# A sandwich layer on one core: three biases moved from TensorE to VectorE and GpSimd, idle matmuls in the second batch, a new order of slots

## What is computed

```python
x_proj = (ln(x) @ w_in.T + b_in)             # q, k, v; the values' bias is bv
opt = softmax(q @ k.T / 4).sum(keys) * v     # per head; see below
x = x + ln(opt @ w_out.T + b_out)
h = ln(x); base = h @ wi_W.T + wi_b
inter = relu(base + (h @ lora_A[i].T) @ lora_B[i].T)   # i = argmax of the gate
x = x + ln(inter @ wo_W.T + wo_b)
```

## Time and profile before

| | us |
|---|---|
| median of three runs | 548.2 (547.74 to 549.51) |
| the profiled execution | 549.36 |
| its span | 547.60 |
| TensorE busy | 518.1 |
| VectorE busy | 459.9 |
| ScalarE busy | 457.8 |
| GpSimd busy | 332.6 |
| TensorE's granted clock, mean | 0.976 |

### The profile page before, as it was taken

The page is one execution under the profiler, slowest core; times in us unless marked ns, Lnnn a source line. Parts: engine busy times, 40 slices in busy tenths (PEclk is TensorE's granted clock), DMA queues, the critical chain, the costliest instruction groups (busy, mean ns, idle before and its releaser), DMA issues.

```text
span 547.6 us, 8941 instructions
## 1 busy us (share of the span) xinstructions
PE 518.1 (95%) x2785; PEld 418.2 (76%) x2785; DVE 459.9 (84%) x987; ACT 457.8 (84%) x1242; POOL 332.6 (61%) x504
## 2 busy tenths in 40 slices
PE   8988977899999999999999999999999998998995
PEld 6756635577887788787987788787878776767995
DVE  4499888797999989998999899998999889893453
ACT  2499987899989998999989998999899988894230
POOL 8794043414980699339971798159942985597262
PEclk9989988599999999999999999999999999999999
DMA  6493353006230544017220625044401740310011
GB/s 247 144 243 97 101 132 77 1 1 173 69 107 1 132 100 135 20 43 189 68 89 1 159 73 154 1 115 117 115 1 31 186 132 0 78 38 2 1 40 39
DMA packets 22535, 47.24 MB, mean 86 GB/s; under 512 B 5237, under 2 KB 13557, under 8 KB 21848
## 3 DMA queue, kind: packets, MB, share of 16 engines
q1 hardware_dynamic: 21800, 45.56, 31.4%
q10 hardware_dynamic: 432, 0.59, 0.3%
q0 software_dynamic: 256, 0.52, 0.3%
HBM read 7.85 MB, written 4.19 MB: 22 GB/s over the span
## 4 chain that ended last, share of the span: by engine, by line
PE 48%; POOL 29%; ACT 10%; DVE 6%; issue 4%; DMA 1%; SPq 0%; POOLq 0%; DVEq 0%
PE pu L193 26%; PE ps L222 10%; ACT ps L519 8%; POOL y L1018 6%; POOL nmr L1012 5%; POOL inter L1078 4%; PE ps L193 4%; POOL xb L1024 4%; POOL vo L1055 3%; DVE nmax L738 2%; POOL xn L1018 2%; PE pu L227 2%; POOL inter L1076 2%; PE pu L314 2%; POOL nmr L1010 2%
## 5 line engine op out<-in xcount | busy, mean ns | idle before, releaser
L519 ACT ACTIVATE ps<-ps,nmax 128x512 f32<-128x512 f32 x512 | 343.9, 698 | 24.7 <-DVE nmax L738 24.1
L738 DVE TENSOR_REDUCE nmax<-ps 128x1 f32<-128x512 f32 x512 | 321.2, 681 | 34.4 <-PE ps L222 33.8
L222 PE MATMUL ps<-stack 128*128 128x512 f32 x512 | 176.2, 422 | 11.3 <-ACT ps L519 9.4
L222 PEld LDWEIGHTS ps<-stack 128*128 128x128 f32 x512 | 93.4, 193 | 49.5 <-ACT ps L519 34.5
L519 ACT ACTIVATION_READ_ACCUMULATOR ps<-ps,nmax 128x1 f32 x512 | 125.0, 244 | 0.0
L193 PE MATMUL pu<-yT,wi_r 128*128 128x512 f32 x336 | 87.8, 397 | 0.0
L193 PE MATMUL pu<-wo_r,inter 128*128 128x256 f32 x648 | 85.3, 285 | 0.0
L193 PEld LDWEIGHTS pu<-wo_r,inter 128*128 128x128 f32 x648 | 81.0, 189 | 1.5
L193 PEld LDWEIGHTS pu<-yT,wi_r 128*128 128x128 f32 x336 | 62.9, 189 | 13.6
L1032 POOL TENSOR_TENSOR ml<-gs,g 128x128 f32<-128x128 f32 (+1 forms) x9 | 3.6, 402 | 104.2 <-DVE g L878 104.2
L1078 POOL TENSOR_TENSOR inter<-y,inter 128x1024 fp32r<-128x1024 f32 x26 | 62.0, 2386 | 2.1
(11 more groups left out here) (150 smaller groups left out, 684.7 us busy)
## 6 DMA issues: line engine op xcount, KB each, us to landing
stack<-qk SPq DMA_DIRECT2D x256, 128.0 KB, 2.5
xb<-in_x SPq DMA_DIRECT2D x7, 512.0 KB, 3.6
out_y<-xb SPq DMA_DIRECT2D x7, 512.0 KB, 3.6
xb<-in_wo SPq DMA_DIRECT2D x1, 1024.0 KB, 5.9
vo<-in_wi SPq DMA_DIRECT2D x2, 512.0 KB, 5.8
oT<-in_wqk ACTq DMA_DIRECT2D x1, 512.0 KB, 4.1
xb<-in_x SPq DMA_DIRECT2D x4, 128.0 KB, 4.1
stack<-qk SPq DMA_DIRECT2D x8, 64.0 KB, 2.1
```

What stands on the lines that cost most here:

```text
L222: e.matmul(ps[i % NS][:], st[:, 1 - p, c, t * 128:(t + 1) * 128], st[:, 2, c, :], start=True, stop=True).then_inc(scored, 1)
L519: e.activation(ps[i % NS][:], ps[i % NS][:], ACT.Exp, bias=nmax[:, i % 8:i % 8 + 1], accum_out=ssum[:, b % 2, t, h:h + 1]).then_inc(exped, 1)
L738: e.tensor_reduce(nmax[:, i % 8:i % 8 + 1], ps[i % NS][:], AX_X, ALU.max, negate=True).then_inc(maxed, 1)
```

## The change

- The bias matmuls of `value`, `project`, `f2` and `f2_last` go, 32, 32, 28 and 4 of them, with `br_r`, its splitting and its DMA. The biases come as an input already spread over 128 partitions, `bf` [128, 3, 256], by a DMA of SP's queue that stands ahead of the first stack DMAs.
- VectorE's copy of the projection (`project` in `vector`) becomes an add of `bf[:, 1]` spread over two tiles.
- GpSimd adds the values' bias (`v_bias`, four adds a batch, behind `sum_norm`) and the second layer's (`y2_bias`, two adds each half, behind that). `scale` and `y2_stats` wait for them. In the last batch's own second layer VectorE adds it as it reads the bank (`last_stats`), and ScalarE's `f2_last` goes.
- Idle matmuls: slots 32 to 63, those of the second batch, can have them too; `FULL` now lists 24 slots. The first batch has them in 26 slots (24 before), the second in 14, two matmuls each.
- The slots are re-ordered on TensorE, ScalarE and VectorE, most in the last batch. In the others `f1(b-1, 6)` goes from slot 30 to the head of the next batch, both turns of y stand behind slot 14, and the statistics of the sum and of the second layer stand one and four slots later.

```diff
-IDLE, FULL = (25, 6, 4), (7, 8, 12, 13, 15, 27, 28, 30)
+IDLE, FULL = (25, 6, 4), (15, 16, 18, 19, 20, 21, 34, 35, 36, 37, 38, 47, 48, 49, 50, 51, 52, 53, 55, 56, 57,
+                           59, 61, 62)
...
-                    if 2 <= g < PAIRS + 2 and g - 2 not in FULL:
+                    if 2 <= g < 2 * PAIRS + 2 and g - 2 not in FULL:
                         run_idle(ps[i % NS], 1)
...
-                    three(o, lambda a, c: xnT[:, a, c, t * 128:(t + 1) * 128], lambda a, c: wv_r[:, a, c, :],
-                          (0, 1), True, False)
-                    p = e.matmul(o, ones_r[:], br_r[:, BV], start=False, stop=True)
+                    p = three(o, lambda a, c: xnT[:, a, c, t * 128:(t + 1) * 128], lambda a, c: wv_r[:, a, c, :],
+                              (0, 1), True, True)
...
-                f1(b - 2, 7), slot(0)
+                f1(b - 2, 6), f1(b - 2, 7), slot(0)
...
-                slot(13), y_t(b - 1, 0)
-                slot(14), y_t(b - 1, 1), q_k(b + 1, 0)
+                slot(13)
+                slot(14), y_t(b - 1, 0), y_t(b - 1, 1), q_k(b + 1, 0)
...
-                slot(14), f2(b - 2, 1), y_t(b - 1, 0)
-                slot(15), y_t(b - 1, 1)
-                slot(16), q_k(b + 1, 0)
+                slot(14), f2(b - 2, 1), y_t(b - 1, 0), y_t(b - 1, 1)
+                slot(15), q_k(b + 1, 0)
+                slot(16)
...
-                    e.tensor_copy(flat(y[:, 2 * u:2 * u + 2, :]), bank_of["y", b, u][:]).then_inc(y_here, 1)
+                    e.tensor_tensor(y[:, 2 * u:2 * u + 2, :], parts(bank_of["y", b, u]),
+                                    bf[:, 1, :].unsqueeze(1).to_broadcast([128, 2, D]), ALU.add).then_inc(y_here, 1)
...
-                            e.wait_ge(y2_here, 2 * b + t // 2 + 1)
+                            e.wait_ge(y2_whole, 4 * b + 2 * (t // 2) + 2)
...
+                e.wait_ge(f2_tile_ps, t + 1)
+                e.tensor_tensor(y2[:, t, :], bank_of["f2", B - 1, t][:, 0:256], bf[:, 2, :],
+                                ALU.add).then_inc(y2_tile_here, 1)
...
-                slot(13), y2_stats(b - 2, HALVES[0]), x_t(b + 1, 1)
+                slot(17), y2_stats(b - 2, HALVES[0]), q_k(b + 1, 2)
...
+            def v_bias(b):
+                e.wait_ge(v_here, 2 * b + 2)
+                for t in ALL:
+                    e.tensor_tensor(vo[:, b % 2, t, :], vo[:, b % 2, t, :], bf[:, 0, :], ALU.add).then_inc(v_whole, 1)
+
+            def y2_bias(b, u):
+                if here(b):
+                    e.wait_ge(y2_here, 2 * b + u + 1)
+                    for t in HALVES[u]:
+                        e.tensor_tensor(y2[:, t, :], y2[:, t, :], bf[:, 2, :], ALU.add).then_inc(y2_whole, 1)
...
-                y_norm(b - 1, HALVES[1]), sum_norm(b - 1, HALVES[0]), sum_norm(b - 1, HALVES[1]), mask(b - 1)
-                y2_norm(b - 2), f1_lows(b - 1, 0, 0), f1_lows(b - 1, 0, 1)
+                y_norm(b - 1, HALVES[1]), sum_norm(b - 1, HALVES[0]), sum_norm(b - 1, HALVES[1]), v_bias(b)
+                y2_bias(b - 2, 0), y2_bias(b - 2, 1), mask(b - 1), y2_norm(b - 2), f1_lows(b - 1, 0, 0)
+                f1_lows(b - 1, 0, 1)
...
-            e.wait_ge(rows_split, 6)
-            e.dma_start(br_r[1:2].bitcast(F32), rows_low.bitcast(F32)).then_inc(rows_moved, 16)
+            e.dma_start(bf[:], bfree).then_inc(bf_loaded, 16)
             first_piece(e, 0, 0)
```

More of the change, by code:

```diff
@@ L271, in project @@
                     for c in range(2):
-                        e.matmul(o, oT[:, c, t * 128:(t + 1) * 128], wout_s[:, c, :], start=c == 0, stop=False)
-                    p = e.matmul(o, ones_r[:], br_r[:, BO], start=False, stop=True)
+                        p = e.matmul(o, oT[:, c, t * 128:(t + 1) * 128], wout_s[:, c, :], start=c == 0, stop=c == 1)
                     if k:
@@ L323, in f2 @@
                         e.wait_ge(f1_pool_low, 4 * b + 2 * part + 2)
-                    three(o, lambda a, f: inter[:, a, f, t * 128:(t + 1) * 128], lambda a, f: wo_r[:, a, f, :],
-                          range(4 * part, 4 * part + 4), part == 0, False)
-                    if part:
-                        p = e.matmul(o, ones_r[:], br_r[:, BW], start=False, stop=True)
-                        if k:
-                            p.then_inc(f2_ps, 1)
-                            filling.clear()
+                    p = three(o, lambda a, f: inter[:, a, f, t * 128:(t + 1) * 128], lambda a, f: wo_r[:, a, f, :],
+                              range(4 * part, 4 * part + 4), part == 0, part == 1)
+                    if part and k:
+                        p.then_inc(f2_ps, 1)
+                        filling.clear()
             def turn_half(name, src, b, h, left, there, wait):
@@ L394, in f2_last @@
                 three(bank[:, 0:256], lambda a, f: inter[:, a, f, t * 128:(t + 1) * 128], lambda a, f: wo_r[:, a, f, :],
-                      range(8), True, False)
-                e.matmul(bank[:, 0:256], ones_r[:], br_r[:, BW], start=False, stop=True).then_inc(f2_tile_ps, 1)
+                      range(8), True, True).then_inc(f2_tile_ps, 1)
             e.wait_ge(const_set, 1)
@@ L454, in tensor @@
                 slot(29), f1(b - 1, 5)
-                slot(30), f1(b - 1, 6)
+                slot(30)
                 slot(31)
@@ L479, in tensor @@
[L479 to L487 removed]
+            slot(3), project(b - 1, 2)
+            slot(4), f2(b - 2, 0, 0), project(b - 1, 3)
+            slot(5)
@@ new lines, in tensor @@
+            slot(6), f2(b - 2, 0, 1)
+            slot(7), f2(b - 2, 1, 0), f2(b - 2, 1, 1)
+            slot(8)
+            slot(9), f2(b - 2, 2, 0), f2(b - 2, 2, 1)
+            slot(10)
+            slot(11), f2(b - 2, 3, 0)
+            slot(12), y_t(b - 1, 0), y_t(b - 1, 1)
+            slot(13)
+            slot(14), gate(b - 1)
+            slot(15), gate_t(b - 1), f2(b - 2, 3, 1)
+            slot(16), o_half(0), project(b, 0)
+            slot(17), masked_t(b - 1)
+            slot(18), project(b, 1)
@@ L499, in tensor @@
[L499 to L504 removed]
+            slot(28), y_half(0), f1(b - 1, 6)
@@ L702, in scalar @@
             slot(8)
-            slot(9)
-            slot(10), f2(b - 2, 0)
+            slot(9), f2(b - 2, 0)
+            slot(10)
             slot(11)
             slot(12)
-            slot(13), y_t(b - 1, 0)
-            slot(14), y_t(b - 1, 1)
-            slot(15)
-            slot(16), gate(b - 1)
-            slot(17), logits(b - 1), gate_exp(b - 1)
-            slot(18), f2(b - 2, 1), o_half(0)
+            slot(13), y_t(b - 1, 0), y_t(b - 1, 1)
+            slot(14)
+            slot(15), gate(b - 1), logits(b - 1)
+            slot(16), f2(b - 2, 1), gate_exp(b - 1)
+            slot(17), o_half(0)
+            slot(18)
             slot(19), masked_t(b - 1)
```

221 lines of the change are left out of this document (95 added, 126 removed).

## The result

| | before | after |
|---|---|---|
| median (runs; lowest to highest) | 548.86 us (4; 547.74 to 550.20) | 540.54 us (4; 540.20 to 541.58) |
| profiled execution, its span | 549.36, 547.6 us | 541.58, 539.8 us |
| mean granted clock in it | 0.976 | 0.991 |
| up to batch 1's scaling | 75.19 us | 73.08 us |
| batch 1 | 63.33 us | 58.82 us |

The ratio is 0.9846, with a 95% interval of 0.9824 to 0.9869: 8.3 us of 548.9 are gone. The stretches begin and end where the prediction put them, at GpSimd's first instruction of `scale`; from one such instant to the next is called the period of a steady batch. The windows of the kernel after, with the same columns as the earlier trace rows: up to batch 1's scaling from the first exponential on, batch 1, a steady batch, the last batch's slots, the tail.

A forecast was written before the change was run, and what follows sets the result against it. The prediction took a ring through GpSimd, TensorE, ScalarE and VectorE, not TensorE alone, to bound the steady batches. Gains of 1.5 + 5.7 + 3.0 = 10.2 us from 548.2 gave 538.0 us, range 532.0 to 543.5.

The forecast's parts named there:

- The ring: Batches 2 to 6: GpSimd, TensorE, ScalarE and VectorE wait in a circle; removing products gains 1.5 us, bounds 0 and 2.2.
- Rival 1: Steady batches: TensorE is the bound after all, giving 7.2 us in place of 1.5, thus 532.3 us; chance 0.20.
- The sign named at the end of the prediction: Prediction is wrong if ScalarE's stretch from the turn of y to the last exp isn't near 30.5 us.
- Rival 3: GpSimd's adds cost double through blocking with VectorE, 12 us over batches 2 to 7, thus 550.0 us; chance 0.07.
- Batch 1: Batch 1: idle matmuls hold the clock, the turn of y comes earlier; gain 5.7 us, bounds 3 and 7.
- rival 2: Batch 1: idle matmuls don't hold the clock; it gives 2.8 or 1 us, thus 540.9 or 542.7; chance 0.19.
- Start and batch 0: Start and first batch: rows' split and DMA gone, new SP transfer, idle matmuls moved; all costed at nothing.
- None of which ends last: Start: the removed rows' split, DMA through SP and TensorE wait don't end last; costed at nothing.
- Moving idle matmuls between its slots costs nothing there: Batch 0: ScalarE is busy 48.67 of 51.19 us, so moving idle matmuls costs nothing, 0.5 either way.
- Last batch and tail: Last batch's slots 1.8 us, ten bias products off the tail's path 1.2 us; sum 3.0, bounds 1.2 and 5.
- The 1.8 us of the slots: Last batch: re-ordered slots let the mask start some 1.6 us earlier (0 to 2.5); 1.8 us taken for it.
- rival 4: Batch 1's gains are lost again to new waits in re-ordered slots; total within 0.3% of 548.2 us; chance 0.05.

The follow-up runs named there:

- experiment 5: Kernel after with two more GpSimd adds in each of batches 2 to 6, between y_norm and sum_norm, ahead of the turn of y; 551.24 us, ratio 1.0045.
- 6: Kernel after with two more GpSimd adds in each of batches 2 to 6, behind the second layer's bias adds, where GpSimd waits for the gate; 540.55 us.
- experiment 3: Kernel before with all bias products left out of TensorE and nothing put in their place; 545.19 us, ratio 0.9939.
- experiment 10: Kernel after with products of ones and zeros at the old bias products' places, except the first batch's values and last batch's last four; 544.96 us, ratio 0.9910.
- 12: Kernel after with slots 17 to 21 back in the old order in its first seven batches; 541.47 us, ratio 0.9853.
- 8: Kernel after without GpSimd's bias add for the second half of batch 5's second layer, which stood in the last batch's slots; 540.67 us, ratio 0.9843.
- 1: Kernel before with the idle matmuls of batch 1 added and nothing else; 547.45 us, ratio 0.9975.
- 4: Kernel before without the bias rows' load, split, second DMA and waits, the bias products kept with a zero row; 549.11 us, ratio 1.0007.
- 11: Kernel before with the new choice of idle matmuls in its first and second batch, nothing else; 545.92 us, ratio 0.9950.
- experiment 9: Kernel after with GpSimd's norm of x moved behind the values' bias adds and VectorE's statistics for it behind slot 12; 545.75 us, ratio 0.9940.

## Why the prediction was right or wrong

The forecast was 538.0 us, a gain of 10.2; the result is 540.5, a gain of 8.3. The total lies in the range and near the forecast, but only one of the terms was right for the reason given; that it came so near is luck, since errors of both signs took each other back.

**The ring.** Predicted 1.5 us for five batches, measured 1.8. That the ring and not TensorE bounds these batches is shown from both sides: work put into it costs its whole length (experiment 5), work beside it nothing (6), and twelve products less on TensorE bring nothing (3). Rival 1 fell with that. The size of 0.3 us per batch was right, but most of it was not the gift of the freed TensorE: in the old order the products' removal gives 0.00. From ScalarE's turn to the ratio it takes 30.89 us in the old order, 30.69 in the new one with products (10) and 30.57 in the new one without. So of 0.32 us a batch about 0.20 come from the new slots alone and 0.12 from the removal, and this only once the slots are moved; slots 17 to 21 hold at most 0.05 of it (12). The step that failed is "So a TensorE that is further ahead can give back up to 0.4 us per batch". The sign named at the end of the prediction held: ScalarE's stretch from the turn of y to the end of the last exponential took 30.25 us, before 30.58.

**GpSimd's adds and VectorE's.** Right: 738 and 744 ns for 736 predicted, no wait of VectorE for them in the steady batches, and the add of the projection took 670 ns where the copy of the earlier trace rows took 692. Rival 3 had no ground in the steady batches; in the last batch the blocking held the mask up by 1.1 us (8), within the 1.5 that the prediction allowed.

**Batch 1.** Predicted 5.7 us, measured 4.5. The clock did what was said, so rival 2 fell. The turn of y comes 25.58 us behind the scaling, before 28.20: 2.6 us, with 3.1 predicted, since the statistics came 11.9 and not 11.2 us behind the scaling. From there on 33.24 us, before 35.13: 1.9 us and not 2.6, because I took a steady batch's stretch for it. What is more, the 63.33 us of before were one draw: the same batch took 60.74 and 60.86 us in other executions. Of the gain in the profiled pair some 3.5 us are the clock (1), of which a typical run gets less, and about 1 us is the new order with the products gone (59.8 to 58.8).

**Start and batch 0.** Predicted 0, measured 2.1: the largest miss in the other direction. Two steps failed. "None of which ends last" was right for the rows' split and DMA (4), but I didn't ask the same of the first batch's four products; they hold the first exponential up by 0.6 to 2.1 us (4 executions against 10). "Moving idle matmuls between its slots costs nothing there" was wrong in two ways: the old choice filled TensorE where the projections run, 1.76 us for eight matmuls, and in three of four executions the clock fell just there, for 1.0 to 1.2 us more (11). The profile of before is the one in which it didn't, so no part of the 0.9 us that it lost to the kernel after is that fall of the clock. From the first exponential on, three of the four executions with it took 51.95 to 52.45 us and the profile of before 50.88; with the new choice it was 49.66 to 50.36 in nine of nine (experiment 9, which adds work there, apart).

**Last batch and tail.** Predicted 3.0 us, measured 0.6 in the wrong direction. The tail's ten products were sized right: 1.26 us in experiment 3 for 1.2. The new order gives them back: it puts the first half's gate transposes ahead of the turn of the second half's values, TensorE idles 2.35 us in three gaps, and the clock fell in six of eight executions, for 1.5 us (3 in experiment 10, its six products included). In the two where it held, the tail was 0.9 us shorter than before. The 1.8 us of the slots failed entirely: the first scaling comes at 32.01 us in the batch instead of 30.43, since its ratio now stands one slot later on VectorE, behind slot 16 and the gate's first step, and the mask at 35.15 instead of 35.65. From the mask to the second scaling it takes 26.45 us instead of 26.07. I had moved the mask by the slots written down and not followed what VectorE had to finish before it; and of a mask 1.1 us earlier only 0.3 arrives at the second scaling, because GpSimd then waits for ScalarE (8). This is rival 4 in the small: a gain lost to a wait in the new order.

So the errors were: 2.1 us not seen at the start, 0.3 too little in the ring, 1.2 too much in batch 1, 3.6 too much at the end. They add up to 2.4 us less gain than forecast. The profiled executions give 7.8 us for the kernel, the medians 8.3. Four runs of before had the median 548.9; the 30 later ones had 549.4.

## What to carry to other kernels

Before an edit is priced on the busiest engine, find the ring (the chain of engines that wait for one another and that comes round once per batch) that closes without slack, and test it with one cheap operation inside and one beside it: the same 1.55 us of GpSimd cost 1.5 us or more a batch or nothing. A ring has neighbours that are almost as long, so moving work out of it pays only if no engine that is full at the new place receives any of it. Matmuls that only hold the clock are free just where TensorE has room. Waits that the edit makes longer, or short gaps close together, can lose the clock in some executions, so a gain of one profiled pair has to be held against the spread of many runs.

## What the runs showed of the hardware that was not expected

The clock can fall after three gaps of only 0.65, 0.92 and 0.78 us with little work between them, in five of seven executions in which this stage has the same instructions; the following eight matmuls then take 2.84 to 3.55 us instead of 1.96. In experiment 5 it fell at the turn of y in three of five like batches of one execution, each time after one wait of 2.2 to 2.4 us; in the other two, after the same wait, it held. A whole kernel's time goes with such draws: the 30 runs of before go from 545.9 to 551.2 us with mean clocks of 0.976 to 0.989.

Four bias products of 0.12 us on TensorE came with an SP queue that took 5.96 to 6.53 us instead of 5.18 or 5.19 to issue its first eight stack DMAs. Why is not shown.
